# Transposed queries moved by DMA instead of TensorE, with the engines' orders and the opening rewritten

## The reference, cut to what matters

```python
h = relu(x @ W1[lang] + b1)                      # 64 hidden features, weights chosen by lang[b]
u = x + h @ W2[lang] + b2
n = layernorm(u) * gamma[lang] + beta[lang]
q = (n @ Wq.T).reshape(b, t, 16, 16)             # 16 heads of 16
k, v = n @ Wk.T, n @ Wv.T                        # one key and value head for all
logits = einsum('btnh,bsh->bnts', q, k) / 4      # causal mask, softmax over s
out = einsum('bnts,bsh->btnh', probs, v).reshape(b, t, 256)
x = x + out @ Wf.T + bf
x = x + ffn(cond2(x))                            # a gelu layer of 1024, then a gated four-layer ffn
```

## Time and profile before

| | us |
|---|---|
| median of three runs | 1155.56 |
| profiled execution, its own time | 1157.74 |
| profiled execution, span of its trace | 1156.00 |
| TensorE busy | 1117.5 (97%) |
| VectorE busy | 804.4 (70%) |
| ScalarE busy | 594.7 (51%) |
| GpSimd busy | 214.6 (19%) |

### The profile page before, as it was taken

One profiled execution on the slowest core, in us unless ns is written; L12 is line 12 of the kernel. 1 busy time (PEld: TensorE's weight loads), 2 busy tenths in 40 slices (PEclk: granted clock), 3 DMA queues, 4 the chain that ended last, 5 costly groups with the idle time before them and its releaser, 6 DMA issues.

```text
span 1156.0 us, 18793 instructions
## 1 busy us (share of the span) xinstructions
PE 1117.5 (97%) x6148; PEld 892.6 (77%) x6178; DVE 804.4 (70%) x1440; ACT 594.7 (51%) x989; POOL 214.6 (19%) x266
## 2 busy tenths in 40 slices
PE   4899999999998999999999999999999999999998
PEld 3567777777775788888888888888888888888886
DVE  2877777776776557756577875778656887568875
ACT  1355655555555634533365654556445565455653
POOL 2233333343345444452000000000000000000000
PEclk9999999999999999999999999999999999999999
DMA  4342122122143456654515443044440444304420
GB/s 122 111 149 60 53 59 63 48 60 63 47 160 124 151 187 202 227 188 150 204 35 164 140 167 115 10 164 146 162 137 0 163 146 163 137 8 145 145 91 37
DMA packets 66765, 135.97 MB, mean 118 GB/s; under 512 B 13793, under 2 KB 28017, under 8 KB 66545
## 3 DMA queue, kind: packets, MB, share of 16 engines
q1 hardware_dynamic: 57696, 114.49, 30.5%
q10 hardware_dynamic: 9024, 20.97, 5.0%
HBM read 107.65 MB, written 30.41 MB: 119 GB/s over the span
## 4 chain that ended last, share of the span: by engine, by line
PE 89%; DVE 6%; SPq 2%; issue 1%; DMA 1%; ACT 1%; POOL 0%; DVEq 0%; POOLq 0%; ACTq 0%
PE bank L1531 35%; PE bank L1493 10%; PE bank L1319 7%; PE bank L1543 5%; PE bank L1469 4%; PE bank L1463 4%; PE bank L1253 4%; PE bank L1234 3%; DVE neg_max L891 2%; PE bank L1274 2%; PE bank L1311 2%; PE bank L1216 2%; PE bank L1200 2%; PE bank L1237 1%; PE bank L1189 1%
## 5 line engine op out<-in xcount | busy, mean ns | idle before, releaser
L1531 PE MATMUL bank<-op_lo,w_ring 128*128 128x512 f32 x896 | 348.6, 389 | 0.0
L1531 PE MATMUL bank<-op_hi,w_ring 128*128 128x512 f32 x896 | 348.6, 389 | 0.0
L1066 DVE TENSOR_TENSOR op_lo<-x_blk,op_hi 128x512 fp32r<-128x512 f32 x288 | 193.8, 684 | 30.4 <-ACT op_hi L764 30.3
L764 ACT ACTIVATE op_hi<-x_blk 128x512 fp32r<-128x512 f32 x288 | 162.8, 620 | 73.6 <-PE bank L1531 69.3
L1531 PEld LDWEIGHTS bank<-op_lo,w_ring 128*128 128x128 f32 x896 | 168.2, 188 | 34.9
L1531 PEld LDWEIGHTS bank<-op_hi,w_ring 128*128 128x128 f32 x896 | 168.2, 188 | 34.9
L891 DVE TENSOR_REDUCE neg_max<-bank 128x2 f32<-128x512 f32 (+1 forms) x192 | 126.0, 685 | 48.0 <-remote 39.7
L617 ACT ACTIVATE p<-bank 128x512 f32<-128x512 f32 x192 | 111.3, 599 | 71.9 <-PE bank L1253 68.2
L788 ACT ACTIVATE x_blk<-x_blk,scales 128x512 f32<-128x512 f32 x96 | 69.3, 722 | 67.0 <-DVE x_blk L1119 28.9
L1493 PE MATMUL bank<-tile_hi,ffn_w 128*128 128x512 f32 x256 | 101.5, 396 | 0.0
L1493 PE MATMUL bank<-tile_lo,ffn_w 128*128 128x512 f32 x256 | 101.5, 396 | 0.0
(11 more groups left out here) (124 smaller groups left out, 1850.0 us busy)
## 6 DMA issues: line engine op xcount, KB each, us to landing
w_ring<-hid_scratch SPq DMA_DIRECT2D x112, 512.0 KB, 4.6
hid_scratch<-comb ACTq DMA_DIRECT2D x8, 1792.0 KB, 7.6
...
xt<-in_x_t SPq DMA_DIRECT2D x16, 256.0 KB
xtok<-in_x_tok SPq DMA_DIRECT2D x16, 256.0 KB
resid<-in_x_t SPq DMA_DIRECT2D x16, 256.0 KB, 3.1
x_scratch<-x SPq DMA_DIRECT2D x16, 256.0 KB, 2.6
...
```

The lines of the kernel that those rows point to most:

```text
L764: nc.scalar.activation(op_hi[:, o % OP_RING, k], x_blk[:, operand_home(o), k], ACT.Copy).then_inc(s["op_hi"], 1)
L1066: nc.vector.tensor_tensor(op_lo[:, o % OP_RING, k], x_blk[:, operand_home(o), k], op_hi[:, o % OP_RING, k].bitcast(F32), ALU.subtract).the ...
L1531: last = mm(banks[first_bank + m][:, :], w, read(v[:, q % OP_RING, k, :]), start=k == 0 and v is op_hi and i not in (P2, P3), stop=k == KB ...
```

## The change

- Queries are projected transposed: `project_queries` now has the weight as the stationary operand and gives head features as rows, all tokens as 256 columns, in one bank (two row blocks, even and odd heads, by a new column order of `w_q`). ScalarE writes the scaled high part (`queries_high`, 512 columns), VectorE the low part (`queries_low`, 512 columns), and SP moves them into `q_t` with six DMAs an element (`move_queries`): each writes 16 rows of 8 KB from 128 rows of 1 KB, 128 KB in all. The 16 transposes, the four copies to `q_t`, `queries_of` and `high_again` are gone.
- Keys and values come from one projection (`w_kv`, values in rows that the keys leave free). ScalarE copies it (`keys_copied`) and writes both key halves (`keys_high`, two of 256 columns), VectorE subtracts (`keys_low`, two of 32 rows), TensorE transposes the values (`values_transposed`, two) and VectorE copies them (`values_of`, two). GpSimd keeps only `rstd_of` and `causal` (and `combine`).
- `q_t`, `keys` and `values` have three buffers instead of two, and the hardware loop three steps instead of two.
- The order of every engine in an iteration is new; the change's description calls it written for transfers of nine microseconds. SP's is: inputs of b + 3, queries of b + 2, store of b - 1, maxima of b + 1, residual input of b. Iteration 14 stores the first block of combined weights after the maxima have been moved instead of before (`finish_chunk` is split into `store_chunk` and `check_chunk`).
- The opening: ScalarE issues three of the first loads, an activation loads ScalarE's table early, nine matmuls of 512 columns on zeros run on TensorE before the data is there, and iteration -1 has an order of its own.

The core of the diff. Of the three `iteration` functions only the new order is shown (lines with + or a blank); the old ones stand in the kernel above.

```diff
-            iteration(-1, 1, True, True, False, False)
+            iteration(-1, 2, True, True, False, False)
             iteration(0, 0, True, True, True, False)
-            with eng.Fori(0, (B - 4) // 2) as pair:
-                for step in (1, 2):
-                    iteration(2 * pair + step, step % 2, True, True, True, True)
+            with eng.Fori(0, (B - 4) // SLOTS) as third:
+                for step in (1, 2, 3):
+                    iteration(SLOTS * third + step, step % SLOTS, True, True, True, True)
             iteration(B - 3, 1, True, True, True, True)
-            iteration(B - 2, 0, False, True, True, True)
-            iteration(B - 1, 1, False, False, True, True)
+            iteration(B - 2, 2, False, True, True, True)
+            iteration(B - 1, 0, False, False, True, True)
...
+            def move_queries(n, slot):
+                sp.wait_ge(s["q_low"], n + 1)
+                settle(sp, "sp_settled")
+                for i, part in enumerate((q_high, q_rest, q_high)):
+                    for par in range(2):
+                        row = SLOT * par + HD * i
+                        sp.dma_start(q_t[slot][row:row + HD, :, :].bitcast(F32), part[:, par, :].bitcast(F32)).then_inc(s["q_moved"], 16)
...
             store_ffn()
-            with sp.Fori(0, (B - 4) // 2) as pair:
-                for step in (1, 2):
-                    b = 2 * pair + step
-                    load_front(b + 3)
+            with sp.Fori(0, (B - 4) // SLOTS) as third:
+                for step in (1, 2, 3):
+                    b = SLOTS * third + step
+                    l = language(b + 3)
+                    load_inputs(b + 3, l)
+                    load_rest(b + 3, l)
+                    move_queries(b + 2, (step + 2) % SLOTS)
                     store_x1(b - 1)
+                    move_maxima(b + 1, (step + 1) % SLOTS)
                     load_resid(b)
-                    move_maxima(b + 1, 1 - step % 2)
             sp.wait_ge(s["x1_stored"], HEAD + 16 * BT)
...
+            move_queries(B - 1, (B - 1) % SLOTS)
+            move_maxima(B - 2, (B - 2) % SLOTS)
+            load_resid(B - 3)
             store_x1(B - 4)
-            load_resid(B - 3)
-            move_maxima(B - 2, 0)
             sp.wait_ge(s["fc1_split"], KD)
             sp.dma_start(fc2_raw[:, :, :], fc2_w).then_inc(s["fc2_loaded"], 16)
             sp.dma_start(fc2_bias[:, 0:1], fc2_b[0]).then_inc(s["bias_loaded"], 16)
             for j in range(BT):
                 sp.dma_start(fc2_bias[0:SHARED - P, 1 + j:2 + j], fc2_b[1, 0:SHARED - P]).then_inc(s["bias_loaded"], 16)
+            move_maxima(B - 1, (B - 1) % SLOTS)
+            load_resid(B - 2)
             store_x1(B - 3)
-            load_resid(B - 2)
-            move_maxima(B - 1, 1)
             ids = expert_ids(0)
...
+            def queries_high(n):
+                act.wait_ge(s["q_mm"], n + 1)
+                if not is_first(n):
+                    act.wait_ge(s["q_moved"], 96 * n)
+                nc.scalar.activation(q_high[:, :, :], ring[0][:, :].rearrange("p (a t) -> p a t", a=2), ACT.Copy, scale=QSCALE).then_inc(s["q_hi"], 1)
+            def keys_copied(n):
+                act.wait_ge(s["kv_mm"], n + 1)
+                if not is_first(n):
+                    act.wait_ge(s["keys_out"], 2 * n)
+                nc.scalar.activation(kv[:, :], ring[1][:, 0:T], ACT.Copy).then_inc(s["kv_out"], 1)
+            def keys_high(n, slot):
+                act.wait_ge(s["kv_out"], n + 1)
+                for par in range(2):
+                    nc.scalar.activation(keys[slot][:, par, :], kv[:, :], ACT.Identity,
+                                         bias=key_row[:, 2 * par:2 * par + 1], scale=key_row[:, 2 * par + 1:2 * par + 2]).then_inc(s["keys_hi"], 1)
...
+            def iteration(b, slot, front, maxima, softmax, tail):
+                if not softmax:
+                    hidden(b + 2)
+                    affine(b + 2)
+                    queries_high(b + 2)
+                    keys_copied(b + 2)
+                    keys_high(b + 2, (slot + 2) % SLOTS)
+                    maxima_out(b + 1)
+                    return
                 if front:
                     hidden(b + 2)
                 if tail:
                     products_out(b - 1, False)
                     products_out(b - 1, True)
+                if softmax and not maxima:
+                    act.wait_ge(s["maxima_moved"], 64 * B)
+                    store_chunk(0)
+                if softmax:
+                    exponential(b, 0)
+                    exponential(b, 1)
+                    exponential(b, 2)
+                    exponential(b, 3)
                 if front:
                     affine(b + 2)
+                if softmax:
+                    exponential(b, 4)
+                if front:
+                    queries_high(b + 2)
+                if softmax:
+                    exponential(b, 5)
+                    exponential(b, 6)
+                    exponential(b, 7)
                 if tail:
                     attention_out(b - 1)
+                if front:
+                    keys_copied(b + 2)
+                if softmax:
+                    exponential(b, 8)
+                    exponential(b, 9)
+                if front:
+                    keys_high(b + 2, (slot + 2) % SLOTS)
                 if maxima:
                     maxima_out(b + 1)
+                if softmax:
+                    exponential(b, 10)
+                    exponential(b, 11)
                 if maxima and not front:
...
+            l = act.value_load(lang[0:1, 0:1], min_val=0, max_val=L - 1)
+            act.wait_ge(s["row_made"], 2)
+            act.dma_start(w1c[:, :, 0:A], cond_w1[bass.ds(l, 1)].rearrange("a p k h -> p (a k) h")).then_inc(s["front_loaded"], 16)
+            act.dma_start(w2c[:, :], cond_w2[bass.ds(l, 1)].rearrange("a p h -> p (a h)")).then_inc(s["front_loaded"], 16)
+            act.dma_start(vec[:, :], cond_vec[bass.ds(l, 1)].rearrange("a p c -> p (a c)")).then_inc(s["front_loaded"], 16)
+            act.wait_ge(s["warm_made"], 1)
+            nc.scalar.activation(warm_row[0:1, :], warm[0:1, 1, 0:1], ACT.Relu)
             act.wait_ge(s["front_loaded"], 80)
             hidden(0)
             affine(0)
+            act.wait_ge(s["const_loaded"], 112)
+            queries_high(0)
+            keys_copied(0)
...
+            def keys_low(n, slot):
+                dve.wait_ge(s["keys_hi"], 2 * (n + 1))
+                for par, rows in enumerate((slice(32, 64), slice(96, 128))):
+                    nc.vector.tensor_tensor(keys[slot][rows, par, :], kv[rows, :], keys[slot][rows, par, :].bitcast(F32),
+                                            ALU.subtract).then_inc(s["keys_out"], 1)
+            def queries_low(n):
+                dve.wait_ge(s["q_hi"], n + 1)
+                nc.vector.scalar_tensor_tensor(out=q_rest[:, :, :], in0=ring[0][:, :].rearrange("p (a t) -> p a t", a=2), scalar=QSCALE,
+                                               in1=q_high[:, :, :].bitcast(F32), op0=ALU.mult, op1=ALU.subtract).then_inc(s["q_low"], 1)
+            def values_of(n, slot):
+                dve.wait_ge(s["v_t_mm"], n + 1)
+                if n in (0, 1, 2) if isinstance(n, int) else False:
+                    dve.wait_ge(s["const_made"], 3 + 2 * SLOTS)
+                src, at = ring[1][:, T:2 * T].rearrange("p (t c) -> p t c", t=NT), 0
+                for row, rows in V_ROWS:
+                    nc.vector.tensor_copy(values[slot][:, :, at:at + rows], src[:, :, row:row + rows]).then_inc(s["values_out"], 1)
+                    at += rows
...
+            def iteration(b, slot, front, maxima, softmax, tail):
+                if not softmax:
+                    split_fc1(0)
+                    add_adapted(b + 2)
+                    normalise(b + 2)
+                    queries_low(b + 2)
...
+                    split_maxima(b + 1)
+                    return
                 if not tail:
                     split_fc1(b + 1)
                 if front:
                     add_adapted(b + 2)
                 elif maxima:
...
                 if maxima:
+                    maximum(b + 1, 0)
+                    maximum(b + 1, 1)
+                if tail:
+                    attention(b - 1, 0)
+                if front:
+                    normalise(b + 2)
+                if maxima:
                     maximum(b + 1, 2)
                     maximum(b + 1, 3)
                 if tail:
+                    attention(b - 1, 1)
                 if maxima:
                     maximum(b + 1, 4)
+                    maximum(b + 1, 5)
+                    maximum(b + 1, 6)
+                if front:
+                    queries_low(b + 2)
                 if maxima:
+                    maximum(b + 1, 7)
+                    maximum(b + 1, 8)
+                    maximum(b + 1, 9)
                     maximum(b + 1, 10)
                     maximum(b + 1, 11)
```

(100 more changed lines are left out.)

391 lines of the change are left out of this document (139 added, 252 removed).

## The result

The changed kernel takes 1146.44 us (median of 4 runs, 1143.6 to 1147.57), the kernel before 1156.15 in the same session (4 runs): a ratio of 0.9898, 95% interval 0.9878 to 0.9918. It is faster by 1.0%, where 2.5% was forecast, and lies above the range. The profiled execution took 1147.46 us with a span of 1145.7.

What follows compares the result with a forecast made beforehand. TensorE, busy 98% of the loop, was taken to bound the kernel; stretch terms -2.5, -3.0, -2.0, -18.0, -2.1 and -0.9 summed to -28.5 us, span 1156.0 to 1127.5, median forecast 1127.1 us, range 1117 to 1144.

Steps and rivals of the forecast that it cites:

- The iteration: Full loop iteration: removed transposes and shorter projections take 1.63 us off TensorE, 21.55 becomes 19.92 an element.
- The cover of the queries: Loop: slack between the query moves' landing (21 to 23.1 us) and the next iteration's ask at 24.4, 1.3 to 3 us.
- lace: Rival, loop: closely chained ScalarE, TensorE and VectorE steps stop each other, half the gain goes, 20.7 an element, 1138; 22%.
- late maxima: Rival, loop: maxima land behind the queries' packets, TensorE waits at `scores` 0, 0.85 us an element, 1139; 10%.
- late queries: Loop, within the slower rival: TensorE waits at `max_scores` 0 if queries take over 10.3 us from `queries_low` to landing.
- The slower rival: Queries late in every element: above 10.3 us each microsecond costs one an element; 13 us gives 1165; slower or undone 9%.
- Element 1 to 2: Stretch between first `scores` of elements 1 and 2: 21.93 to 19.9, -2.0 us.
- `vec` lands near 6, -1.9: Opening: `vec`, issued from ScalarE's queue, lands near 6 instead of 7.82 us, gaining 1.9.
- Warmed, -2.4: Opening: first adapter's four matmuls fall from 2.06 us toward 0.81 warm; it and its pair give -2.4.
- SP's line: Element 0 to 1: six query moves of element 2, four maxima moves, then landing set the length; 18.0 us, -3.0.
- the walk: Stepping through the new order with traced durations: everything issued in 19.5 us, without the trace's stalls; as a rival 1119, 9%.
- the wait for ScalarE's copies: Element 14 to 15: `products_transposed` waits for product copies behind `check_chunk`, 2.7 us, replacing the 2.78 us maxima stall.

Runs made afterwards that it cites:

- Twelve pieces: Changed kernel with the 3 MB HBM-to-HBM copy of the third phase's input issued as twelve pieces, one per loop iteration 1 to 12: 1137.89 us.
- the constants held back: Changed kernel with SP issuing constants and later loads only after the first five loads have landed: 1144.05 us.
- kept busy: Changed kernel with matmuls on unused data through the opening (28 for 9 at the start, 16 and 20 more later): 1136.14 us.
- the first run with late maxima: Changed kernel with the last element's maxima moved only after SP has read the experts' numbers: 1143.51 us.
- The parts measured alone: Separate kernels against the changed one: constants held back 1144.05 us, TensorE kept busy 1136.14 us, fc1 split behind maxima plus four early maxima units, first scores at 56.34 us.
- together: Changed kernel with copy pieces, held constants, extra matmuls (11 at the start), new maxima order, and 3 MB load behind iteration 13's store: 1131.55 us, ratio 0.977.
- the new order gave nothing: Order edit on the changed kernel: fc1 split behind element 0's maxima, four maxima units ahead of element 1's queries; alone, first scores at 56.34 us.

## Why the prediction was wrong

**The iteration: right.** 19.92 by subtraction, 19.72 measured; the rest is old stalls, kept in the sum, that went. The cover of the queries was forecast at 1.3 to 3 us and is about 1.7 (8.7 us from first issue to landing); SP's six issues take 3.9 for 4.3. None of the rivals on the loop happened: no lace (TensorE's only wait is half a microsecond for VectorE's residual), no late maxima (0.66 us more of delay cost nothing), no late queries. The slower rival's price was too low: a wait of 4.4 us costs 6.7, not 4.4.

**Element 1 to 2: the step that failed first, 9.3 us.** The prediction took "19.9" as for any full iteration. It priced the moves that the new loop issues, but not what the new order does to the 3 MB copy. Before, the copy had landed (77.4) when `vec` was issued (79.25); now it goes out behind six moves and four loads, is under way until 97.1, and `vec`, issued at 88.50, lands at 100.52. The 7.18 us of wait and the slow rate behind it make the 9.3. Twelve pieces gave 9.4 back.

**The opening: 12.7 us.** Four terms failed. "`vec` lands near 6, -1.9" counted the place in the queue, not the bytes beside it: it landed at 9.40, and at 6.06 with the constants held back; 3.2 us. "Warmed, -2.4" was nothing, since TensorE stood for four microseconds behind its nine matmuls; kept busy, it gave 6.9, so the slow rate was a larger item than was forecast, in the projections and not only in the adapter. The forecast had the maxima start at 29 to 32, and they started at 38.63. That is 29.1 us from the adapter's start, and 23.1 with TensorE kept busy, which is the lower end of the forecast (23 to 26 from 6): the order was priced rightly for a fast TensorE, and the slow rate costs 6.0 where the range had 3.

And from there to `scores` 15 to 16.5 were forecast and 20.0 taken. The sum has 9.8 us of VectorE's work and 5.45 from the last maximum on. In the trace VectorE starts its first maximum 1.8 us behind TensorE's first unit, which runs at the slow rate, and stands 1.5 us for the third, behind element 1's keys and values on TensorE, then 0.53 and 0.46 for units at the slow rate (the last four are 0.91 apart for 0.68). Behind the transposes of the maxima it isn't the moves that end last but TensorE's own work, element 2's adapter and two units at the slow rate: 6.15 us and no wait for a move, 5.04 with a wait of 1.16 for one in the first run with late maxima, where the clock was up.

The parts measured alone (3.2, 6.9, 2.1) sum to 12.2; together they gave 8.0, where the new order gave nothing once TensorE was fast, and element 0's projection of queries ran slow again (3.36 for 1.99 us). Matmuls and held constants without the new order were not tried.

**Element 0 to 1: 3.6 us.** SP's line (moves, then landing) was to end it in 18.0. No `scores` waits for a move there; TensorE's own work ends it, and its length goes with the granted clock: 19.03 at 1.00 (the first run with late maxima), 19.64 at 0.99, 21.11 at 0.89, 21.55 at 0.86, as here. So 2.5 of the miss is the clock, 1.0 the walk.

**Element 13 to 14: 2.0 us better.** The trace of before has waits of 1.31, 0.53 and 0.48 there, on `norm`, `keys` and the maxima; all are gone (two of 0.38 and 0.33 come), where the forecast took 0.5 for them (2.1 less the iteration's 1.63). **Element 14 to 15: right in its time**, partly by luck: the wait for ScalarE's copies is 1.0, not 2.7, and 1.2 for GpSimd's mask and 1.0 for VectorE's maxima, which the sum doesn't have, make up for it.

**The rest: 2.6 better.** "The last 783 us have nothing of the change in them" overlooked that they begin behind the wait of the earlier trace rows. The new order removes that wait, and with it, most likely, the slow clock behind it, 2.0 of the 2.6; the other 0.6 stay open.
